# Attention inside a macaron block: two heads side by side in the rows of the TensorE array, rows moved in one hop

## The reference

```python
# B=8, L=512, C=256, H=16, D=16, HIDDEN=768
x = x + 0.5 * ffn(layernorm(x))          # ffn: (silu(x Wg^T) * (x Wu^T)) Wd^T, int8 weights / 127
qh, kh, vh = heads(xn @ Wq.T), heads(xn @ Wk.T), heads(xn @ Wv.T)      # xn = layernorm(x)
scores = einsum('bhld,bhsd->bhls', qh, kh) / 4 - slope[h] * abs(s - l)
x = x + merge(softmax(scores) @ vh) @ Wo.T + bo
x = x + 0.5 * ffn(layernorm(x))
```

## Time and profile before

| | us |
|---|---|
| time, median of three runs (lowest, highest) | 903.22 (902.56, 903.54) |
| profiled execution, its own time | 903.27 |
| its span | 901.5 |
| PE busy / VectorE / ScalarE / GpSimd | 842.3 / 653.9 / 527.9 / 427.2 |
| maxima by VectorE (L885), 512 of them | 341.3 |
| maxima products on PE, 512 | 222.6 |
| score products on PE, 512 | 159.3 |
| value products on PE, 1024 records | 136.9 |
| moved by DMA | 85.24 MB |

### The profile page before, as it was taken

The page is one execution under the profiler, slowest core; times in us unless marked ns, Lnnn a source line. Parts: engine busy times, 40 slices in busy tenths (PEclk is TensorE's granted clock), DMA queues, the critical chain, the costliest instruction groups (busy, mean ns, idle before and its releaser), DMA issues.

```text
span 901.5 us, 13262 instructions
## 1 busy us (share of the span) xinstructions
PE 842.3 (93%) x4672; PEld 577.1 (64%) x4672; DVE 653.9 (73%) x1359; ACT 527.9 (59%) x745; POOL 427.2 (47%) x486
## 2 busy tenths in 40 slices
PE   3899999869999999999999999999998998999997
PEld 2788888734655665665665565565564446888886
DVE  6799888477677677777677677677778725677874
ACT  4344434415658668758758767767766684444443
POOL 0444434423635645645644644644644465334443
PEclk9999999967999999999999999999999999999999
DMA  9220000274482482482482482383383000010001
GB/s 384 72 76 13 2 3 3 49 213 115 96 224 58 105 221 53 100 225 54 95 223 61 90 228 60 85 225 68 81 227 70 1 2 2 26 49 26 25 26 48
DMA packets 37086, 85.24 MB, mean 95 GB/s; under 512 B 3746, under 2 KB 4770, under 8 KB 36818
## 3 DMA queue, kind: packets, MB, share of 16 engines
q1 hardware_dynamic: 36482, 83.45, 34.8%
q10 hardware_dynamic: 512, 0.53, 0.2%
HBM read 45.68 MB, written 38.87 MB: 94 GB/s over the span
## 4 chain that ended last, share of the span: by engine, by line
PE 76%; DVE 9%; DMA 8%; ACT 2%; issue 2%; SPq 1%; POOL 1%; ACTq 0%; DVEq 0%
PE ps L975 70%; DVE row_max L885 4%; DMA k_aug<-parts_scratch 3%; DMA q_aug<-max_row 3%; DMA parts_scratch<-parts 2%; DVE hid L781 1%; PE ps L987 1%; PE ps L1031 1%; PE ps L1026 1%; ACT gated L588 1%; PE ps L1012 1%; PE ps L1036 1%; DVE max_in L896 1%; DVE w_max L838 1%; SPq L425 0%
## 5 line engine op out<-in xcount | busy, mean ns | idle before, releaser
L885 DVE TENSOR_REDUCE row_max<-ps 128x1 f32<-128x512 f32 x512 | 341.3, 687 | 123.6 <-PE ps L975 122.0
L676 ACT ACTIVATE probs<-ps 128x1024 f32<-128x1024 f32 x256 | 252.5, 1022 | 96.5 <-PE ps L975 95.0
L553 POOL TENSOR_TENSOR probs<-probs,diag 128x256 f32<-128x256 f32 x256 | 187.7, 736 | 230.9 <-ACT probs L676 230.6
L975 PE MATMUL ps<-k_aug,q_aug 96*128 96x512 f32 x512 | 222.6, 459 | 12.4 <-DVE row_max L885 6.2
L486 POOL TENSOR_TENSOR hid_r<-hid,hid_r 128x512 fp32r<-128x512 f32 x96 | 124.6, 1299 | 172.8 <-ACT hid_r L582 171.4
L975 PE MATMUL ps<-xnt,wgu_r 128*128 128x512 f32 x768 | 187.5, 399 | 14.6 <-DVE hid L781 10.4
L975 PEld LDWEIGHTS ps<-k_aug,q_aug 96*128 96x128 f32 x512 | 95.6, 194 | 145.7 <-DVE row_max L885 118.7
L975 PEld LDWEIGHTS ps<-xnt,wgu_r 128*128 128x128 f32 x768 | 144.4, 192 | 52.3 <-DVE hid L781 17.6
L975 PE MATMUL ps<-q_aug,k_aug 98*128 98x512 f32 x512 | 159.3, 404 | 6.1 <-DMA q_aug<-max_row 6.0
L975 PE MATMUL ps<-probs,v_aug 128*32 128x512 f32 x1024 | 136.9, 607 | 0.8 <-POOL probs L553 0.8
L588 ACT ACTIVATE gated<-ps 128x512 f32<-128x512 f32 x96 | 57.6, 600 | 114.4 <-PE ps L975 114.4
(11 more groups left out here) (62 smaller groups left out, 690.4 us busy)
## 6 DMA issues: line engine op xcount, KB each, us to landing
parts_scratch<-parts SPq DMA_DIRECT2D x128, 256.0 KB, 5.9
q_aug<-parts_scratch SPq DMA_DIRECT2D x32, 512.0 KB, 4.9
k_aug<-parts_scratch SPq DMA_DIRECT2D x32, 512.0 KB, 6.6
x_sb<-x_in SPq DMA_DIRECT2D x8, 512.0 KB, 12.7
x_out<-x_sb SPq DMA_DIRECT2D x8, 512.0 KB, 2.6
wgu_i<-w_gate_up SPq DMA_DIRECT2D x2, 768.0 KB, 6.2
k_aug<-k_rows_scratch SPq DMA_DIRECT2D x1, 1088.0 KB
w_att<-w_att SPq DMA_DIRECT2D x1, 1024.0 KB, 11.5
```

Source lines behind the costliest of these rows:

```text
L553: nc.gpsimd.tensor_tensor(tile, tile, diag[:, n * QH + 2 * pair:n * QH + 2 * pair + 2, :], ALU.mult).then_inc(fixed, 1)
L676: nc.scalar.activation(probs[:, kt % 2, 2 * pair:2 * pair + 2, :], ps[:, at:at + 2, :], ACT.Exp).then_inc(exp_done, 1)
L885: nc.vector.reduce_max(row_max[:, quad % 2, u % TT, u // TT:u // TT + 1], max_bank(b, tile)[0], mybir.AxisListType.X).then_inc(s1_used, 1)
L975: return nc.tensor.matmul(out, lhs, rhs, start=start, stop=stop, **k)
```

## The change

- **Three terms instead of four, six segments instead of eight.** A head now fills 48 + 12 rows, with its maximum 62. The bias terms need no low parts: slopes are divided by the slope of head 0 for even heads (`SLOPE_UNITS`), so that they are powers of two, the scale goes into q (`q_scale`) and comes back as the scale of the exponent. The diagonal table now covers two tiles (2 MB instead of 1).
- **Two heads in one set of partitions.** `q_aug` and `k_aug` hold pairs of heads: one from partition 0 on, the other from partition 64 on (`GROUP`). The products on 60 or 62 rows therefore address tiles of 64 rows x 128 columns at row 0 and row 64; all others keep 128 x 128 (values 128 x 32). Maxima tiles go in pairs too, `u % 2` chooses the row group, and `spread_tiles` deals out even numbers.
- **Two of each.** There are now two `q_aug` and two `k_aug`, one for even and one for odd elements; the rows of the next element are free when the turn before has made its last scores.
- **One hop.** The columns of Wq and Wk are sorted on the host so that the projection has the rows in the order wanted, and SyncE copies them straight from `parts` to their places (`move_rows`, 24 DMAs of 128 KB a turn). `parts` has one place instead of two, so ScalarE's split waits until the rows of the chunk before are moved (`rows_moved`).
- **Maxima in one transpose.** A quad's maxima are transposed in one product of 128 columns; ScalarE copies 32 x 128 and issues two DMAs of 16 rows.
- **New places** for the fills and new weights for the deal; VectorE applies the kept normalization in steps 2 to 5 of quad 1, four tiles ahead of time.

```diff
-    (0, 3): "heads3_prev", (0, 5): "max1", (0, 6): "xt0_next", (0, 7): "xt1_next",
+    (0, 0): "xt0_next", (0, 1): "xt1_next", (0, 3): "heads3_prev", (0, 4): "max1", (0, 5): "qk0_next",
...
-WEIGHTS = {"heads": 2, "max": 2, "turn": 2, "xt": 2, "qk": 6, "v": 6, "out": 6}
+WEIGHTS = {"heads": 0.6, "max": 0.2, "turn": 0.55, "xt": 0.55, "qk": 1.4, "v": 1.7, "out": 1.7}
...
-            until = int(MAX_TILES * done / whole + 1e-6)
+            until = 2 * int(MAX_TILES // 2 * done / whole + 1e-6)
...
-        q_aug = sb("q_aug", [P, H, L], F32R)
+        q_aug = [sb(f"q_aug{side}", [P, NP, L], F32R) for side in range(2)]
...
+            def move_rows(b, name):
+
+                seq, kind, part = fill_parts(b, name)
+                chunk, is_k = part // 2, part % 2
+                wait_done(sp, b, name)
+                pairs = slice(chunk * NP // CHUNKS, (chunk + 1) * NP // CHUNKS)
+                for i in range(2):
+                    for term, half in enumerate((0, 0, 1) if is_k else (0, 1, 0)):
+                        at = i * GROUP + term * D
+                        to = (k_aug if is_k else q_aug)[seq % 2][at:at + D, pairs, :].bitcast(F32)
+                        sp.dma_start(to.rearrange("p q t -> p (q t)"),
+                                     parts[i * GROUP:(i + 1) * GROUP, is_k, half, :].bitcast(F32)
+                                     ).then_inc(rows_moved[is_k], 16)
...
-                        if kind == "qk" and not (isinstance(seq, int) and seq == 0):
-                            act.wait_ge(parts_out, (NQ * PUTS) * seq)
+                        if kind == "qk":
+                            wait(act, rows_moved[part % 2], (seq * CHUNKS + part // 2) * MOVES)
...
                 elif kind == "max":
                     if halves[0] == 0:
                         pe.wait_ge(neg_ready, seq * NQ + part + 1)
-                    for t in tiles:
-                        ins = nc.tensor.transpose(bank[0:2 * QH, t * P:(t + 1) * P], max_in[:, t, :], eye[:])
+                    if halves[0] == 0:
+                        ins = nc.tensor.transpose(bank[0:2 * TT * QH, 0:P], max_in[:].rearrange("p i o j t -> p (i o j t)"), eye[:])
...
-                    matmul(bank, q_aug[0:ROW_MAX, h, t * P:(t + 1) * P], k_aug[0:ROW_MAX, h, :],
-                           True, True).then_inc(s1_done, 1)
+                    matmul(bank, q_aug[seq % 2][rows:rows + ROW_MAX, pair, t * P:(t + 1) * P],
+                           k_aug[seq % 2][rows:rows + ROW_MAX, pair, :], True, True).then_inc(s1_done, 1)
...
                         for i in range(2):
-                            h = n * QH + 2 * pair + i
-                            ins = matmul(ps[:, scores_at + 2 * pair + i, :], k_aug[0:ROWS, h, kt * P:(kt + 1) * P],
-                                         q_aug[0:ROWS, h, :], True, True)
+                            rows = slice(i * GROUP, i * GROUP + ROWS)
+                            ins = matmul(ps[:, scores_at + 2 * pair + i, :],
+                                         k_aug[b % 2][rows, 2 * n + pair, kt * P:(kt + 1) * P],
+                                         q_aug[b % 2][rows, 2 * n + pair, :], True, True)
```

More of the change, by code:

```diff
@@ new lines, in tables @@
+    diag = np.zeros((P, 2, H, P), np.float32)
+    for e in range(2):
+        at = e * P + np.arange(P)
+        far = np.abs(at - centre[half[at] // 2])
+        over = (half[at][None, :] == half[at][:, None]) & (far[None, :] > far[:, None])
+        excess = np.where(over, 2.0 * np.abs(at[None, :] - at[:, None]), 0.0)
+        by_head = -slopes().astype(np.float64)[HEADS_IN_ORDER]
+        diag[:, e] = np.exp(by_head[None, :, None] * excess[:, None, :])
+    scale = np.array([D ** -0.5 / np.float32(SLOPE_UNITS[p % 2]) for p in range(P)], np.float32).reshape(P, 1)
@@ L458, in _, with lay_rows @@
-            turns(sp, turn)
+            def lay_rows(side):
+                for i in range(2):
+                    sp.dma_start(q_aug[side][i * GROUP + ROW_BIAS:i * GROUP + ROW_MAX, :, :].bitcast(F32), d_qrows[i]
+                                 ).then_inc(aug_in[side], 16)
+                    sp.dma_start(k_aug[side][i * GROUP + ROW_BIAS:i * GROUP + ROWS, :, :].bitcast(F32),
+                                 d_krows.rearrange("r (o t) -> r o t", o=1).to_broadcast([ROWS - ROW_BIAS, NP, L])
+                                 ).then_inc(aug_in[side], 16)
@@ L460, in store @@
+            lay_rows(0)
+            for part in range(4):
+                move_rows(-1, f"qk{part}_next")
+            sp.wait_ge(ffn[0]["y_used"], 2 * B)
+            lay_rows(1)
+            for b in range(B - 1):
+                wait(sp, st_done, b * (NQ * STEPS))
+                for part in range(4):
+                    move_rows(b, f"qk{part}_next")
             def store(b):
@@ L1178, in turn @@
                             made += count
-            turns(pe, turn)
+            for b in range(B):
+                turn(b)
             weigh_values(B * NQ - 1, NQ - 1, TT - 1, B - 1)
```

269 lines of the change are left out of this document (116 added, 153 removed), and 3 rows, old and new, of the table FILLS.

## The result

| | before | after |
|---|---|---|
| time, median (lowest, highest), us | 902.89 (902.10, 903.54) | 929.02 (926.95, 931.79) |
| ratio to before, 95% interval | | 1.0292 [1.0261, 1.0323] |
| span of the profiled execution, us | 901.5 | 928.3 |
| to the first exponents | 209.0 | 213.3 |
| the first seven turns | 476.0 | 494.8 |

The kernel became slower by 2.9%, where 864 us were forecast; the time lies outside the range too. The seven turns took 18.8 us more instead of 31 less, and each of the other three parts is longer as well. Some executions of a kernel are a few per cent longer throughout, at a lower clock: every ratio in this document leaves them out, the medians of b1, a1, c1 and e3 contain them, and the traces of b1 and e3 are of such executions, so of these two only turns at a granted clock of 1.00 are read.

What follows compares the result with a forecast made beforehand. PE (TensorE) was taken to bound the kernel, VectorE's maxima to hold it afterwards. Turn 51.2 + 9.8 + 2.7 = 63.7 us against 68.1: -31 over seven turns, -5.5 last turn, -3 way in; 903.2 - 39.5 = 864 us, range 832 to 904.

Steps and rivals of the forecast that it cites:

- "I take nothing" for the changes of form: Entering and leaving 64-row form around pairs, 38 changes a turn: counted as free, upper bound 9.4 us.
- no overlap and free changes: Rival (2), chance 0.07: paired products run one after the other, changes cost nothing; turn 68.6 us, total 903.
- no overlap and drains: Rival (3), chance 0.07: pairs don't overlap and each change drains the array; turn 75.2 us, total 954.
- overlap and drains: Pairs run side by side but changes of form drain the array; turn 68.7 us.
- overlap and free: The forecast itself, chance 0.45: pairs take 0.24 us and changes cost nothing; turn 63.7 us.
- Rival (1): Changes of form drain the array while pairs overlap: 888 to 901 us, say 895; chance 0.23.
- The way in: Before the first attention turn: one hop instead of two brings rows sooner, -3 us (bounds 0 and -5).
- The loop with VectorE: Pairs wait for VectorE's maxima to free two banks: 9.8 us of new waits a turn, 5.4 at PE's other end.
- Rival (4): The wait for VectorE's maxima costs half: turn 58.8 us, total 828; chance 0.13.
- New places: Moved fills in a turn: q/k fills close together, output two steps after the turn it needs; +0.8 us.
- Transposes: A quad's maxima go through one transpose instead of four on PE: 1.3 us saved a turn.
- The second load behind a value group: A pair after the values waits for two weight loads: +1.4 us a turn, nothing if both go at once.

Runs made afterwards that it cites:

- b1: Kernel before with maxima products reading 64 rows instead of 96, bias table zero; 1048.95 us, ratio 1.1383.
- a1: Changed kernel with both products of each pair on the first 64 rows, so they can't overlap; 991.13 us, ratio 1.0938.
- c1: Changed kernel with both products of a pair reading rows 0 to 65: no overlap, no form change except at the values; 963.01 us, ratio 1.0662.
- e3: c1 with the maxima dealt one at a time instead of in pairs; 936.85 us, ratio 1.0281.
- a4: Changed kernel with VectorE's kept normalization moved from quad 1 to the same steps of quad 3; 923.07 us, ratio 1.0243.
- e2: Kernel before with one pause of PE a turn, the values in quad 1 waiting for later exponents; 945.85 us, ratio 1.0457.
- f2: Changed kernel with the output's first half moved to quad 1 step 4 and GpSimd's bias addition to quad 2 step 1; 909.78 us, ratio 1.0059.
- g1: f2 with the kept normalization also moved to quad 3, three moves in all; 913.01 us, ratio 1.0088.
- e1: Kernel before with only a quad's maxima transposed in one product instead of four; 903.38 us, ratio 0.9993.

## Why the prediction was wrong

**The step that failed first: "I take nothing" for the changes of form.** The order gave 38 a turn, and the bounds were nothing and 9.4 us. b1 has 0.20 for a single one, and c1 to a1 gives 5.0 for all 38. The argument against a cost (the columns stay whole) was a guess about what "form" means; the value group was the only evidence, and it spoke for a cost. With the prediction's own terms the third turn (69.8 us, forecast 63.7) now adds up: 51.2 for PE, less 1.4 for a second load that costs nothing, 38 x 0.20 = 7.6 for the changes, 8.9 for VectorE, 0.6 to 1.5 for a stretch of 3.4 us at half clock, and 2.0 to 2.9 left for other waits, which were put at 2.7. The term put at nothing is larger than the whole difference of 6.1 us. The Trainium skill, "TensorEngine Tiling (Array Packing)", Key Properties, had said that a change of tiling mode drains TensorE; the traces now agree for 64 against 128 rows, at 0.20 us, the load that is no longer hidden included.

So the rest of the working inside a turn held well. Four cases were worked out, and each now has a kernel: no overlap and free changes 68.6 (c1: 70.4), no overlap and drains 75.2 (a1: 76.0 at 0.98, 0.6 to 1.5 less without its stretch at half clock; the 72.5 in the prediction's working should be 64.1 + 9.4 = 73.5, which makes it 76.2), overlap and drains 68.7 (the changed kernel: 69.6 at 0.98, so some 68.1 to 69.0), overlap and free 63.7, which none of these kernels can have. Rival (1) was the case, at 0.23.

**Why the total lies 34 us above that rival's 895.** From its upper end, 901 us with +4 in seven turns, -3 in the last and -3 at the way in:

- *Half clock inside turns, some 15 us.* The seven turns took +18.8 instead of +4. By the clock of their windows they hold some 52 us at half clock, where those of the kernel before hold 5, all in the first. What it costs varies: 0.18 of its length in c1, 0.40 between the fourth and the fifth turn (69.6 and 72.3 us, some 6.8 us of it more), 0.44 in a4. For the 47 us more that is 8 to 21 us: enough for the 15, but it doesn't fix them. The seventh turn, the longest, also has the extra work of VectorE and waits 11.4 us for maxima. The prediction took PE's work and waits to be additive. They aren't always: in e2 a wait also slowed the products behind it.
- *The way in, +4.3 instead of -3.* "One hop would land near 182.7" left out SyncE's queue: by the prediction's own 0.62 us an issue and 6.6 to land it would have been near 187. Its twelve issues last from 173.85 to 182.6, and the last of them needs its 6.5 us to land on top. The first maxima are at 189.63, not 185. The four kept rows took 2.7 us between the maxima instead of 1.3.
- *The last turn, +0.7 instead of -3 (or -5.5).* It has the form changes too, and a clock of 0.94.
- *Behind the last turn, +3.0*, counted as nothing. 1.6 us lie ahead of the second element and 0.2 in each after it. "The feed-forwards are the same" doesn't hold: an element of either one takes 18.4 us instead of 18.2, in a1, c1, f2 and g1 too. No run here tells why.

Together 15 + 7 + 4 + 3 = 29, which with 901 makes 930; the profiled execution took 930.13. This splits the difference by place, it doesn't prove the causes.

**Terms that were mis-sized.** *The loop with VectorE*, 9.8 us (5.4 with drains): read from starts it is 8.5 to 9.2 in the second to sixth turn and 0.6 before. That is near the forecast, but with the changes in it 5.4 should have been left, and a deal made to save 4.1 of it saved 1.2: laying out spacings by hand doesn't give the waits of a place. Rival (4), half the loop, was not the case. *New places*, +0.8: the wait for `att_t` alone is 1.5 a turn (12.0 in 8), and the three moves of g1 (66.7) bring some 1.5 to 2 at full clock. *Transposes*, -1.3: -0.5 to -1.0 in a turn (e1). *The second load behind a value group*, +1.4: nothing, both loads go at once, the end that stood beside it.

**What was right.** A pair in 0.24 us, its two products mostly 3 or 4 ns apart; waits of PE for row_max of "some 70" us (74 in eight turns, read from starts, against 8 before); DMA from 85.24 to 43.17 MB and no wait for rows inside a turn; VectorE 51 us busy in a turn.

## What to carry to other kernels

Before two products are packed side by side, count the places where the work around them uses another tiling, and price each with a measured row (here 0.2 us, about what packing one pair saves); packing pays where such products stand together, not where they alternate with others. What an engine saves arrives only if the next one can take it: here 14.3 us of products became 6.4, nearly all of the rest waiting for maxima. And a wait that disappears from the list may have covered another one in the queue of a third engine, so look at what stands in that queue before moving anything.

## What the runs showed of the hardware

- A change between products on 64 and on 128 rows costs 0.20 us in either direction (b1: 0.43 and 0.42 instead of 0.23). Between a value group (32 columns) and a pair it is no dearer than it was: 0.33 from the pair behind the values to the next (359.07 to 359.40), where one product took 0.35.
- Weights for both halves of the rows load at the same time: two loads in 0.19 us. The Trainium skill, "TensorE: Matmul & The Clock Gate", Why this matters for your kernels, has starts within 4 ns for products on different row groups; the trace agrees, with 3 or 4 ns for most pairs of scores.
- The granted clock fell to 0.50 inside turns behind waits of 1.69 and 0.94 us with full work between them, and stayed there for 3.4 us and more; in e2 a pause of 3.5 us did it; in four turns of a4 the wait of 1.7 us alone didn't. Not every such stretch stands behind a wait that the profile names, so its exact condition stays open. It cost 0.18 to 0.44 of its length.
- VectorE's two short steps on the maxima (0.17 us each in the way in) took 0.58 and 1.21 us in the third turn, where GpSimd was multiplying by the table from 374.92 to 375.65 and adding an output from 375.62 to 376.89. Each ended 0.04 us after the GpSimd instruction beside it:

```profile
375.11 0.58 DVE L893 TENSOR_SCALAR max_in<-row_max 128x16 fp32r<-128x16 f32 x1
375.72 1.21 DVE L895 SCALAR_TENSOR_TENSOR max_in<-row_max,max_in 128x16 f32<-128x16 f32 x1
```

The Trainium skill, "GPSIMD Engine Reference", 1. Specifications, says that GpSimd and VectorE share their interfaces to SBUF, with contention when VectorE's instruction has two inputs in SBUF or runs in a mode with two ports. The second of these rows has two such inputs and fits that; the mode of the first is not known, and no run took the two engines apart.
